# Attention kernel with two AdaLN blocks: inverse row sums taken from TensorE to a VectorE transpose and a trip through DRAM, once per pair of heads

## What is computed

```python
h = _layernorm(x) * (1 + ca) + sa
latent_kv = h @ w_kv_down                     # (.., 128)
k, v = split(latent_kv @ w_kv_up)             # 16 heads of 64
q = h @ w_q
att = softmax(causal(q k^T * 64**-0.5))       # 1024 x 1024 per head and batch
y = att @ v
x = x + ga * (y @ w_out)
```

## Time and profile before

| | |
|---|---|
| median of 3 runs | 1795.16 us (1793.74 to 1796.03) |
| the profiled execution | 1797.59 us, its span 1796.3 us |
| PE busy | 1737.0 us, 97% (weight loads 1207.7 us, 67%) |
| DVE busy | 1250.7 us, 70% |
| ACT busy | 887.7 us, 49% |
| POOL busy | 854.0 us, 48% |
| DMA | 164.42 MB, mean 92 GB/s |
| mean granted TensorE clock | 0.999 of 2.4 GHz |

### The profile page before, as it was taken

One profiled execution on the slowest core, in us unless ns is written; L12 is line 12 of the kernel. 1 busy time (PEld: TensorE's weight loads), 2 busy tenths in 40 slices (PEclk: granted clock), 3 DMA queues, 4 the chain that ended last, 5 costly groups with the idle time before them and its releaser, 6 DMA issues.

```text
span 1796.3 us, 40559 instructions
## 1 busy us (share of the span) xinstructions
PE 1737.0 (97%) x16006; PEld 1207.7 (67%) x16006; DVE 1250.7 (70%) x2766; ACT 887.7 (49%) x1968; POOL 854.0 (48%) x1282
## 2 busy tenths in 40 slices
PE   9999999999999999999999999999999999999998
PEld 5666685668566767566856667756685666766667
DVE  5888848626788885753678887675468888676545
ACT  4676634223577763322457775432246767443233
POOL 2777842221187874241138777314114877731410
PEclk9999999999999999999999999999999999999999
DMA  6555570321255554040135555305013555530500
GB/s 185 129 134 127 125 208 31 54 42 37 69 138 128 128 120 149 1 81 15 37 92 131 130 126 122 133 2 95 0 43 103 134 126 124 132 109 2 94 1 25
DMA packets 119915, 164.42 MB, mean 92 GB/s; under 512 B 30032, under 2 KB 86832, under 8 KB 118704
## 3 DMA queue, kind: packets, MB, share of 16 engines
q1 hardware_dynamic: 105760, 155.03, 35.9%
q10 hardware_dynamic: 13968, 6.82, 1.3%
HBM read 63.16 MB, written 4.24 MB: 38 GB/s over the span
## 4 chain that ended last, share of the span: by engine, by line
PE 72%; DVE 14%; ACT 5%; SPq 4%; DMA 3%; issue 1%; POOL 1%; ACTq 0%; DVEq 0%; POOLq 0%
PE scores L466 13%; PE bank L684 10%; PE scores L664 9%; PE bank L719 4%; PE bank L466 4%; SPq L1002 4%; DVE prob L813 3%; ACT prob L924 2%; PE scores L1776 2%; PE scores L1686 2%; PE scores L1114 2%; DMA placed<-prob 2%; PE bank L725 2%; PE bank L721 2%; PE scores L1748 2%; PE scores L437 2%
## 5 line engine op out<-in xcount | busy, mean ns | idle before, releaser
L882 POOL COPY placed<-prob 32x768 f32<-32x768 f32 x384 | 315.5, 822 | 27.5
L297 POOL TENSOR_TENSOR rstd<-rstd,minus_half 128x2 f32<-128x2 f32 x96 | 69.7, 728 | 533.1 <-DVE rstd L296 531.0
L684 PEld LDWEIGHTS bank<-placed,v_t 128*64 128x64 f32 x4608 | 250.0, 137 | 75.7 <-issue 70.5
L684 PE MATMUL bank<-placed,v_t 128*64 128x128 f32 x4608 | 272.7, 275 | 9.9 <-DMA placed<-hx 4.8
L664 PE MATMUL scores<-k_t,q_t 64*128 64x512 f32 (+3 forms) x1536 | 275.1, 496 | 0.8 <-ACT rec_t L934 0.8
L806 DVE CUSTOM_DVE_ANT_0 mod_rows<-scores,hx 128x128 f32<-128x128 f32 (+7 forms) x256 | 191.8, 749 | 75.5 <-PE scores L664 75.5
L813 DVE STREAM_TRANSPOSE prob<-prob 128x1536 f32<-128x1536 f32 x128 | 222.9, 1765 | 27.4 <-ACT prob L924 27.1
L806 DVE CUSTOM_DVE_ANT_0 x<-scores,hx 128x128 f32<-128x128 f32 (+7 forms) x256 | 192.7, 753 | 0.0
L924 ACT ACTIVATE prob<-mod_rows,neg_max 128x128 f32<-128x128 f32 (+2 forms) x192 | 137.3, 715 | 102.9 <-DVE neg_max L806 86.6
L664 PEld LDWEIGHTS scores<-k_t,q_t 64*128 64x128 f32 x1536 | 129.5, 186 | 85.1 <-issue 62.0
L870 POOL COPY rec_wide<-rec 128x128 f32<-128x128 f32 x256 | 65.0, 289 | 226.6 <-DVE rec L817 168.6
(11 more groups left out here) (249 smaller groups left out, 3435.8 us busy)
## 6 DMA issues: line engine op xcount, KB each, us to landing
placed<-prob SPq DMA_DIRECT2D x640, 96.0 KB, 2.2
f<-in_L_ffn_f SPq DMA_DIRECT2D x16, 2048.0 KB, 13.6
placed<-hx SPq DMA_DIRECT2D x320, 96.0 KB, 2.2
mod_rows<-mod_scratch SPq DMA_DIRECT2D x32, 128.0 KB, 4.3
out<-x SPq DMA_DIRECT2D x16, 256.0 KB, 2.2
w_ring<-in_L_attn_w_q ACTq DMA_DIRECT2D x24, 128.0 KB, 2.6
w_ring<-in_L_attn_w_kv_up ACTq DMA_DIRECT2D x48, 64.0 KB, 2.0
next_x<-in_L_attn_x SPq DMA_DIRECT2D x6, 512.0 KB, 4.1
```

The costliest lines, as they stand in the source:

```text
L297: step = pool.do(lambda e, ts=ts: nc.gpsimd.tensor_tensor(rstd[:, ts], rstd[:, ts], minus_half[:, ts], op=ALU.pow), var, filled)
L684: last = nc.tensor.matmul(out_bank[rows_, at_:at_ + P], v_t[pair % 2][:, j, rows_], placed[m % 2][:, :, head, first_block(m, i) + j, :], s ...
L882: nc.gpsimd.tensor_copy(placed[m % 2][target * GROUP:(target + 1) * GROUP, source, :, :, :], prob[m % 3][source * GROUP:(source + 1) * GRO ...
```

## The change

The inverse is made once per pair instead of once per round, and its turning leaves PE:

- ACT's exponentials accumulate into `row_sum[:, pair % 2, head * 8 + tile]`.
- DVE: at the end of a C round, between the two shuffles, one reciprocal of 16 columns (`invert`), and after the second shuffle `turn_inverse`, a transpose of 32x32 blocks of a 128x32 tile.
- ACT: `store_inverse` at the end of a C round issues the store of that tile (16 KB) to `inverse_dram`, in rows of queries.
- SP: `spread_inverse`, behind the moves of the C round, waits for the store and for the norms of the pair before, and loads the rows back as `inverse_wide`, 128 x 1024: each of the two rows of 1024 inverses goes to 64 partitions (512 KB written).
- POOL: `widen` goes; `norm` runs four rounds late (`NORM_LAG = 4`), from `inverse_wide`.
- PE: `turn_inverse` goes, and the wait for `rec_copied` in `scores`; `output_part` takes 6 pairs (`BEGUN`), and the last step for tiles 0 and 1 the last two.
- ACT's `copy_rec` goes.

The projections are as before. The diff, cut to its core:

```diff
+    inverse_dram = nc.dram_tensor("inverse_scratch", [2, 32, P], F32, kind="Internal").ap()
...
-        rec_t = [part("rec_t", [P, 4 * P]), tmp[:, 0:2, :].rearrange("p t n -> p (t n)")]
-        rec_wide = part("rec_wide", [P, 4, P])
+        inverse_wide = part("inverse_wide", [P, S])
+        inverse, inverse_t = tmp[:, 0, 0:32], tmp[:, 0, 32:64]
...
+        NORM_LAG = 4
+        BEGUN = PAIRS - 2
...
-                    if m > 1 and at_ // 512 == SCORE_BANKS - 1:
-                        e.wait_ge(flow["rec_copied"], base["rec_copied"] + m - 1)
...
-            def turn_inverse(m):
-                e.wait_ge(flow["widened"], base["widened"] + m + 1)
-                e.wait_ge(flow["masked"], base["masked"] + parts_through(min(m + 1, ROUNDS - 1)))
-                if m > 0:
-                    e.wait_ge(flow["rec_copied"], base["rec_copied"] + m)
-                for k in range(len(tiles_in(m))):
-                    last = nc.tensor.transpose(rec_bank[:, k * P:(k + 1) * P], rec_wide[:, k, :], ident[:, :])
-                last.then_inc(flow["rec_turned"], 1)
...
-                for j in range(PAIRS - 1):
+                for j in range(BEGUN):
                     nc.tensor.matmul(job_bank[:, tile * D:(tile + 1) * D], yT[:, j, tile * P:(tile + 1) * P], wout[:, j, :],
...
-                if m > 0:
-                    turn_inverse(m - 1)
...
-            def invert(m):
-                k, count = column_of(m, 0, 0), HEADS * len(tiles_in(m))
-                nc.vector.reciprocal(rec[:, k:k + count], row_sum[:, k:k + count]).then_inc(flow["inverted"], 1)
+            def invert(pair):
+                e.wait_ge(flow["exp_done"], base["exp_done"] + PARTS_OF * (pair + 1))
+                nc.vector.reciprocal(inverse[:, 0:HEADS * T], row_sum[:, pair % 2, :]).then_inc(flow["inverted"], 1)
+
+            def turn_inverse(pair):
+                e.wait_ge(flow["inverted"], base["inverted"] + pair + 1)
+                if base["inverse_stored"] + pair:
+                    e.wait_ge(flow["inverse_stored"], base["inverse_stored"] + 16 * pair)
+                nc.vector.transpose(inverse_t, inverse).then_inc(flow["inverse_turned"], 1)
...
             def norm(m):
-                e.wait_ge(flow["kept"], base["kept"] + len(COPIES) * min(m + 2, ROUNDS))
-                e.wait_ge(flow["rec_copied"], base["rec_copied"] + m + 1)
+                pair = m // ROUNDS_OF
+                e.wait_ge(flow["kept"], base["kept"] + len(COPIES) * min(m + NORM_LAG, ROUNDS))
+                e.wait_ge(flow["inverse_spread"], base["inverse_spread"] + 16 * (pair + 1))
                 e.wait_ge(flow["values_read"], base["values_read"] + m + 1)
                 for lo, hi in out_parts(m):
                     dst = out_place(m, lo, hi)
-                    last = nc.gpsimd.tensor_tensor(dst, dst, by_tile(rec_t[m % 2][:, lo * P:hi * P]), op=ALU.mult)
+                    last = nc.gpsimd.tensor_tensor(dst, dst, out_place(m, lo, hi, inverse_wide), op=ALU.mult)
                 last.then_inc(flow["normed"], 1)
...
+            def store_inverse(pair):
+                e.wait_ge(flow["inverse_turned"], base["inverse_turned"] + pair + 1)
+                e.dma_start(inverse_dram[pair % 2].rearrange("k (a i) -> a k i", a=GROUPS), inverse_t
+                            ).then_inc(flow["inverse_stored"], 16)
...
+            def spread_inverse(pair):
+                e.wait_ge(flow["inverse_stored"], base["inverse_stored"] + 16 * (pair + 1))
+                if pair > 0:
+                    e.wait_ge(flow["normed"], base["normed"] + ROUNDS_OF * pair)
+                heads = inverse_dram[pair % 2, 0:HEADS * T, :].rearrange("(h k) i -> h (k i)", h=HEADS)
+                e.dma_start(inverse_wide[:, :], heads.unsqueeze(1).to_broadcast([HEADS, HD0, S])).then_inc(flow["inverse_spread"], 16)
...
+                if m % ROUNDS_OF == ROUNDS_OF - 1:
+                    spread_inverse(m // ROUNDS_OF)
...
-            return lambda e: nc.tensor.matmul(ps, yT[:, PAIRS - 1, t * P:(t + 1) * P], wout[:, PAIRS - 1, :], start=False, stop=True,
-                                              skip_group_check=True)
+                for j in range(first, PAIRS):
+                    last = nc.tensor.matmul(ps, yT[:, j, t * P:(t + 1) * P], wout[:, j, :], start=False, stop=j == PAIRS - 1,
```

More of the change, by code:

```diff
@@ L161, in build @@
     neg_max = sb("neg_max", [P, 16])
-    row_sum = sb("row_sum", [P, 16])
+    row_sum = sb("row_sum", [P, 2, 16])
     rec = sb("rec", [P, HEADS1])
@@ L530, in batch @@
         masked_scores = [a[:, EARLY:T, :].rearrange("p t n -> p (t n)") for a in (mod_rows, x)]
+        if b == 0:
+            pool.do(lambda e: nc.gpsimd.memset(inverse, 0.0))
         cleared_future = pool.do(lambda e: nc.gpsimd.memset(future, 0.0), *carry["h_read"])
@@ L593, in out_parts, with out_place @@
             return [(0, 2)] if len(tiles_in(m)) == 2 else [(0, 3), (3, 4)]
-        def out_place(m, lo, hi):
+        def out_place(m, lo, hi, row=None):
             tiles = sorted(tiles_in(m))
             step = tiles[lo + 1] - tiles[lo] if hi - lo > 1 else 1
-            return by_tile(yT[:, m // ROUNDS_OF, :])[:, tiles[lo]:tiles[hi - 1] + 1:step, :]
+            return by_tile(yT[:, m // ROUNDS_OF, :] if row is None else row)[:, tiles[lo]:tiles[hi - 1] + 1:step, :]
+        NORM_LAG = 4
+        BEGUN = PAIRS - 2
         def by_tile(ap):
@@ L766, in pe_pairs @@
                     return [job(0, j) for j in JOBS[:2]]
-                return values(m) if kind == "values" else turn_inverse(m)
+                return values(m)
             for j in JOBS[2:]:
@@ L855, in dve_pairs @@
                         minimum(m, i, head)
-                for head in range(HEADS):
-                    shuffle(m, head)
-                invert(m)
+                shuffle(m, 0)
+                if m % ROUNDS_OF == ROUNDS_OF - 1:
+                    invert(m // ROUNDS_OF)
+                shuffle(m, 1)
+                if m % ROUNDS_OF == ROUNDS_OF - 1:
+                    turn_inverse(m // ROUNDS_OF)
                 if b == 0 and m == 2:
@@ L897, in pool_pairs @@
                     e.wait_ge(flow["kept"], base["kept"] + len(COPIES) * m)
-                widen(m)
+                if m >= NORM_LAG:
+                    norm(m - NORM_LAG)
                 keep(m)
-                if m > 0:
-                    norm(m - 1)
-            norm(ROUNDS - 1)
+            for m in range(ROUNDS - NORM_LAG, ROUNDS):
+                norm(m)
         def act_pairs(e):
@@ L917, in exponential @@
             def exponential(m, i, head):
-                k = column_of(m, i, head)
+                k, pair, sum_at = column_of(m, i, head), m // ROUNDS_OF, head * T + tiles_in(m)[i]
+                if m % ROUNDS_OF == 0 and i == 0 and head == 0 and pair > 1:
+                    e.wait_ge(flow["inverted"], base["inverted"] + pair - 1)
                 if i == 0 and head == 0 and b * ROUNDS + m > 2:
@@ L1097, in batch, with last_products, emit @@
         SPARE_TMP = 2
-        def last_product(ps, t):
-            return lambda e: nc.tensor.matmul(ps, yT[:, PAIRS - 1, t * P:(t + 1) * P], wout[:, PAIRS - 1, :], start=False, stop=True,
-                                              skip_group_check=True)
+        def last_products(ps, t, first):
+            def emit(e):
+                for j in range(first, PAIRS):
+                    last = nc.tensor.matmul(ps, yT[:, j, t * P:(t + 1) * P], wout[:, j, :], start=False, stop=j == PAIRS - 1,
+                                            skip_group_check=True)
+                return last
+            return emit
         def y_ready(t, pair=PAIRS - 1):
@@ L1118, in head_output @@
             yield
-            done = pe.do(last_product(ps, t), y_ready(t))
+            done = pe.do(last_products(ps, t, PAIRS - 1), y_ready(t))
             read, wrote = residual(t, ps, done, mod_rows[:, 0, :], slot=SPARE_TMP, rows_late=None)
@@ L1126, in head_outputs_begun @@
             for t, ps in zip(tiles, places):
-                done = pe.do(last_product(ps, t), y_ready(t))
+                done = pe.do(last_products(ps, t, BEGUN), y_ready(t))
             written = []
@@ L1519, in batch @@
         next(output3)
-        pe.do(lambda e: pe_pairs(e, ("inverse", ROUNDS - 1)))
         next(output5)
```

28 lines of the change are left out of this document (11 added, 17 removed).

## The result

| | before | changed |
|---|---|---|
| median (4 runs each) | 1794.65 us (1793.74 to 1796.03) | 2073.51 us (2069.59 to 2079.24) |
| ratio, 95% interval | | 1.1556 [1.1527, 1.1584] |
| span of the profiled run | 1796.3 us | 2071.9 us |
| mean granted TensorE clock | 0.999 | 0.943 |
| hardware queue of SP: packets, MB | 105760, 155.03 | 109920, 171.80 |

The account below looks back on a forecast made before the run. PE, busy 97% of the span, was taken as the bound, with SP's moves as second chain. 36.8 us saved less 3.2, 12.0, 2.5 and 3.0 left 16.1, so 1795.2 became 1779 us; range 1767 to 1797.

Parts of the forecast that it names:

- Its transfer, 4.1 us to landing as 512 KB of x take: SP's spread ahead of the A round's moves: 1.9 us of extra transfer, bounds 0 to 1.9 per pair, taken near zero.
- Rival D: Spread fully delays the moves behind it, deciding from 0.7 us a pair on: 17 us slower, 1812 us; chance 0.13.
- End of a batch: Last pair's norms need the last spread: hidden with 2 us to spare; 2 us a batch lost if it doubled.
- SP's place for the issue: Spread's issue of 0.6 us fits between the end of C's moves at 162.1 and A's shuffles at 162.6.
- PE's saving: PE drops 256 transposes: 0.53 after round A, 0.31 after B, 0.31 after C, 1.15 us per pair.
- the ceiling: All of PE's transposes gone: 1.15 us per pair, times 32 pairs, 36.8 us at most.
- 0.5 us later: ACT's store and weight-load issues before the next A round's first exponential delay it; DVE loses 0.5 of 2.5 us waiting.
- the A rounds and the new work: Tighter A rounds plus new work on DVE, ACT and SP once a pair: 3 us lost in all.
- points 1 to 3: Savings PE can't keep: 3.2 us at batch starts, 12.0 in B rounds, 2.5 in round 20.
- point 1: Start of a batch, rounds 0 to 3: DVE comes no sooner, so 4 x 0.8 = 3.2 us lost.
- point 3: Round 20 of each batch: no projections behind it, PE waits for moves; 4 x 0.6 = 2.5 us lost.
- point 2: B rounds: values product waits for SP's moves; 7.6 us in nine rounds, 4.4 in ten others, 12.0 lost.

Follow-up runs that it names:

- the form by head: The changed kernel with the spread as two DMAs, one per head, each with its 64 repeats as slowest dimension; 1784.49 us, ratio to before 0.9939.
- the version of 1776.8 us: The form by head, with ACT issuing the store after two exponentials of the next A round and the weight load after two more; 1776.84 us, ratio 0.9898.
- the version of 1770.2 us: The version of 1776.8 us, with POOL copying 7 of a round's 16 blocks instead of 6 and SP moving 9; 1770.17 us, ratio 0.9846.

## Why the prediction was wrong

The sign, and 290 us, hang on one number: "**Its transfer, 4.1 us to landing as 512 KB of x take**". It took 15.5 us. I priced a transfer by its bytes, from a row of the same size, while the diff showed a source of another form: two rows, each repeated. In the form by head each half lands 4.1 us after its own issue, and the whole 4.9 us in the median after the first one, near what the row said. From that one number follow two of the three marks that I had set for being wrong: A rounds waiting in most pairs, and norms waiting for the spread. The third, a pair without waits that is not shorter by 1.15 us, was met too, for another reason (PE's saving, below).

- *Rival D* had the mechanism (the moves behind the spread are late, decided from 0.7 us a pair on), but its price was capped at "1.9 us per pair", again from the 4.1. The spread landed 15.5 - 4.1 = 11.4 us later than supposed, and 6.3 us of it in the mean reached PE.
- *End of a batch*: "Hidden, with 2 us to spare" became 31.5 / 4 = 7.9 us a batch.
- *No term for the clock.* A wait of 6.81 us cost another 2.3 us in the next product; over the run it was 69 us of 289.
- *SP's place for the issue* held: 163.71, after the moves of C and before those of A.
- *PE's saving* was too large. The 0.53, 0.31 and 0.31, "together 1.15 us per pair", were the distances from the transposes to the scores. But without transposes the scores start later behind the projection than the transposes did. The projections of the pair in the earlier trace rows, before:

```profile
143.13 1.98 PE L721 MATMUL bank<-latT,w_ring 128*128 128x512 f32 x4
...
151.04 2.05 PE L725 MATMUL bank<-w_ring,latT 128*128 128x128 f32 x16
...
158.80 3.70 PE L719 MATMUL bank<-hT,w_ring 128*128 128x512 f32 x8
```

  and in the version of 1776.8 us:

```profile
137.67 2.85 PE L668 MATMUL scores<-k_t,q_t 64*128 64x512 f32 x12
...
143.22 1.98 PE L716 MATMUL bank<-latT,w_ring 128*128 128x512 f32 x4
145.13 2.85 PE L668 MATMUL scores<-k_t,q_t 64*128 64x512 f32 x16
...
150.69 2.05 PE L720 MATMUL bank<-w_ring,latT 128*128 128x128 f32 x16
152.67 2.86 PE L668 MATMUL scores<-k_t,q_t 64*128 64x128 f32 x20
...
158.24 3.70 PE L714 MATMUL bank<-hT,w_ring 128*128 128x512 f32 x8
161.87 0.70 PE L668 MATMUL scores<-k_t,q_t 64*128 64x512 f32 x2
```

  1.91, 1.98 and 3.63 us from projection to scores, against 1.82, 1.89 and 3.54 from projection to the transposes of the earlier trace rows. So 0.27 of the 1.15 us never was to be had. The period of this pair is 161.87 - 137.67 = 24.20 us, 25.06 - 24.20 = 0.86 us shorter, and the ceiling is some 28 us, not 36.8. The distances are the same in the version of 1770.2 us, and neither timeline has a wait there; what makes the scores start later was not seen.
- *ACT*: "0.5 us later" was 1.15, since the store's issue took 0.51 and the weight load's, directly behind it, 0.69, and neither the 0.38 of the earlier trace rows. Moving both is worth 7.7 us, more than the 3 us that I put on the A rounds and the new work together.
- *B rounds and the rest*: with the right access pattern the sum was near by chance. The form by head gained 10.9 us by the medians (12.9 by the profiled spans; the profiled run before lies some 2 us above its median) against 16.1 forecast: a ceiling 9 us too high and ACT's term too low, against losses in points 1 to 3 that were too high. With ACT's issues moved, the profiled spans are 20.9 us apart (the medians 18), so some 7 of the 28 are lost, where points 1 to 3 had 17.7. PE's waits tell where. The longest that is new stands in the first rounds of the first batch, here before and then in the version of 1776.8 us:

```profile
58.74 2.84 PE L684 MATMUL bank<-placed,v_t 128*64 128x128 f32 x48 [1.23 <-ACT q_t L910]
```

```profile
58.67 5.39 PE L688 MATMUL bank<-placed,v_t 128*64 128x128 f32 x48 [3.13 <-ACT q_t L901]
```

  The waits for q_t, all at the start of a batch, grew from 1.6 to 5.3 us, and the product behind this one took 2.6 us more at a granted clock of 0.50: 6.3 us, where point 1 had 3.2. Round 20 (the waits for hx) lost 6.1 - 4.8 = 1.3 us, where point 3 had 2.5. All waits for prob grew from 3.3 to 3.7 us, where point 2 had 12.0 for the B rounds. So the largest loss of my sum hardly exists there.

## What to carry over

Price a DMA by the form of both its sides, not by its bytes: look at the slowest dimension, above all where a few rows are repeated over partitions, and compare with a row of the same form. When a queue is shared, one slow transfer is paid by what is issued behind it. A wait of TensorE can cost more than its length: here 6.81 us of waiting were followed by a product at half the clock. When work leaves an engine, read the saving from the step around it (from the instruction before to the instruction after), not from the removed step's start.

## What the runs showed of the hardware

- A spread of 512 KB whose slowest dimension is 2 was there for the waiting norm 15.5 us after its issue. As two transfers with 64 in that place, each landed after 4.1 (3.5 to 5.3), both 4.9 us after the first issue.
- With the slowest dimension at 4, a 4 KB packet took 0.25 to 0.40 us in the mean of a pair instead of the 0.2 of two engines (the sixteen had 0.19 to 0.31), and hardly anything was won (2035 against 2058 us for two transfers). I had not expected it, and its cause is open.
- After 6.81 us of idle time TensorE's granted clock was 0.50 for the next 4.2 us (5.13 us for a product of 2.84). Over the whole run it was 0.943 with 31 waits for moves of up to 9.0 us, and 0.997 in the form by head, where PE's waits for moves were 1.3 us at most.
- ACT's weight-load issue took 0.69 us directly behind the store's issue and 0.39 with two exponentials between them; the store's took 0.53 us in both places.
